# A decoder of two layers on one core: the first cross-attention's exchanged key halves by SBUF transfers, its sums ahead of the mix, two GpSimd memsets later

## The reference, cut to what matters

```python
x = _layernorm(x + _L0_attn_ref(x, ...))
x = _layernorm(x + _L0_xattn_ref(x, ctx_1024, cos, sin, ...))   # here
x = _layernorm(x + _L0_ffn_ref(x, ...))
...
def apply_rope(x, cos, sin):
    d2 = x.shape[-1] // 2
    x1, x2 = (x[..., :d2], x[..., d2:])
    return jnp.concatenate([x1 * cos - x2 * sin, x2 * cos + x1 * sin], axis=-1)
```

## Time and profile before

| | |
|---|---|
| median of 3 runs | 538.3 us (536.81 to 538.79) |
| the profiled execution | 538.49 us, of which the span is 536.7 us |
| PE busy | 426.9 us, 80% of the span |
| DVE, ACT, POOL busy | 317.9, 205.1, 141.0 us |
| mean granted clock of PE | 0.891 |
| the first cross-attention's loop | some 111 to 226 us of the span |

### The profile page before, as it was taken

How to read it: one execution, slowest core, us unless ns; L and a number is a source line. 1 busy time by engine, 2 the same in 40 slices (tenths; PEclk the granted TensorE clock), 3 DMA queues, 4 the chain that set the end, 5 groups by cost and what they waited for, 6 DMA issues and landing times.

```text
span 536.7 us, 6915 instructions
## 1 busy us (share of the span) xinstructions
PE 426.9 (80%) x2568; PEld 247.9 (46%) x2576; DVE 317.9 (59%) x741; ACT 205.1 (38%) x257; POOL 141.0 (26%) x133
## 2 busy tenths in 40 slices
PE   0628957489999999869999558697377989967994
PEld 0306624244444445546777425444133444544484
DVE  4579944627766765551511477863696776225754
ACT  0555613142333233114333348764133445622800
POOL 3205733337777665430000300000100000001500
PEclk9967977889999999978999875999687999985998
DMA  8511000000004111150051250000000000000000
GB/s 317 196 28 42 2 0 1 1 2 0 1 0 158 40 39 40 37 204 2 33 94 26 40 64 5 3 4 1 0 1 2 2 1 3 1 31 0 1 0 21
DMA packets 7358, 19.36 MB, mean 36 GB/s; under 512 B 1750, under 2 KB 3126, under 8 KB 6806
## 3 DMA queue, kind: packets, MB, share of 16 engines
q1 hardware_dynamic: 7324, 18.91, 12.0%
HBM read 17.26 MB, written 1.15 MB: 34 GB/s over the span
## 4 chain that ended last, share of the span: by engine, by line
PE 42%; DVE 26%; POOL 15%; issue 12%; ACT 3%; DMA 1%; POOLq 0%; another core or an unknown queue 0%; DVEq 0%
PE ps L1190 39%; POOL big L540 7%; DVE ps L1043 4%; POOL big L547 4%; POOL rstd L490 2%; DVE mx_a L1047 2%; DVE stats L773 2%; DVE big L866 2%; DVE ps L861 2%; POOL big L522 1%; DVE normed L783 1%; PE ps L1197 1%; DVE x L783 1%; DVE meanvar L776 1%; PE ps L1553 1%
## 5 line engine op out<-in xcount | busy, mean ns | idle before, releaser
L1190 PE MATMUL ps<-big,late 128*32 128x256 f32 (+4 forms) x792 | 103.3, 386 | 13.8 <-DVE mx_x L1043 4.0
L1190 PE MATMUL ps<-late,big 128*128 128x128 f32 (+1 forms) x448 | 64.8, 277 | 3.8 <-DVE mx_x L1043 2.2
L1190 PEld LDWEIGHTS ps<-big,late 128*32 128x32 f32 (+3 forms) x800 | 39.7, 117 | 55.3 <-issue 26.8
L726 ACT ACTIVATE big<-ps 128x1024 f32<-128x1024 f32 x48 | 49.0, 1023 | 39.9 <-PE ps L1190 39.6
L488 POOL TENSOR_SCALAR vareps<-meanvar 128x4 f32<-128x4 f32 (+1 forms) x11 | 2.5, 229 | 224.9 <-DVE meanvar L776 224.9
L1190 PEld LDWEIGHTS ps<-late,big 128*128 128x128 f32 (+1 forms) x448 | 45.0, 152 | 27.3 <-issue 20.6
L664 ACT ACTIVATE big<-ps 128x1024 f32<-128x1024 f32 x32 | 32.8, 1024 | 64.8 <-PE ps L1190 52.9
L540 POOL TENSOR_TENSOR big<-big 128x512 f32<-128x512 f32 x32 | 40.5, 1267 | 43.3 <-DVE big L926 43.3
L1043 DVE CUSTOM_DVE_ANT_0 ps<-ps,big 128x512 f32<-128x512 f32 x64 | 42.6, 717 | 12.2 <-PE ps L1190 9.0
L926 DVE TENSOR_SCALAR big<-big 128x1024 f32<-128x1024 f32 x32 | 25.4, 793 | 39.8 <-ACT big L664 39.8
L1190 PE MATMUL ps<-big 64*128 64x256 f32 (+1 forms) x320 | 47.4, 410 | 1.7 <-POOL big L547 1.0
(11 more groups left out here) (229 smaller groups left out, 655.4 us busy)
## 6 DMA issues: line engine op xcount, KB each, us to landing
attn_w<-in_w_x SPq DMA_DIRECT2D x1, 2560.0 KB, 13.2
big<-parts_kx SPq DMA_DIRECT2D x18, 128.0 KB
late<-in_w_up SPq DMA_DIRECT2D x1, 2048.0 KB, 7.8
late<-in_w_dn SPq DMA_DIRECT2D x4, 512.0 KB, 3.8
attn_w<-in_w_up SPq DMA_DIRECT2D x1, 1024.0 KB, 7.9
attn_w<-in_w_dn SPq DMA_DIRECT2D x1, 1024.0 KB, 10.3
parts_kx<-ctx_r SPq DMA_DIRECT2D x1, 768.0 KB, 3.2
rowv<-in_rowv SPq DMA_DIRECT2D x1, 576.0 KB, 4.3
```

Of the source, the lines that this page charges most:

```text
L726: nc.scalar.activation(ex1[:, n % 3, :].rearrange("p (r n) -> p r n", r=2), ps[:, 2 * (n % 2):2 * (n % 2) + 2, :], ACT.Exp, scale=scale).t ...
L1190: return nc.tensor.matmul(o, lhsT, rhs, start=start, stop=stop, skip_group_check=shared)
```

## The change

1. The keys are projected once. ACT copies the result from PSUM to a new tile `kc` in SBUF. SP's queue then moves it, by four transfers of 32 rows, into `kt2` with neighbouring blocks of 32 rows exchanged (q to q ^ 1). DVE makes the cosine product from PSUM as before, and the sine product in place on `kt2`, now with both inputs in SBUF. POOL's addition stays. `project0` has the keys of batch 0 at u = 0, the query at u = 1, the keys of batch 1 at u = 2, and nothing at u = 3.
2. The denominators of a batch come one logits step later, ahead of the next mix: (c, 0) at u = 3 and (c-1, 1) at u = 1.
3. The loads of w_up0 and w_dn0 move from SP's queue to ACT's.
4. The two memsets behind post1 wait for `x_k_parts`, which DVE signals after it has split the second cross-attention's keys beside expert 1.
5. Some semaphores are merged.

```diff
         kt2 = big1(3072, [P, 2, CS])
+        kc = mid(4096, [P, 2, CS])
...
-            sp.wait_ge(S["e0_used"], 4 * (NPAIR // 2))
-            sp.dma_start(w_up0, a["w_up0"]).then_inc(ld["e0"], 16)
-            for c in range(NPAIR // 2, NPAIR):
-                e = 2 * c - NPAIR
-                sp.wait_ge(S["e0_used"], 4 * (c + 1))
-                sp.dma_start(w_dn0[:, e:e + 2], a["w_dn0"][:, e:e + 2]).then_inc(ld["dn0"], 16)
+            for n in range(2 * NPAIR):
+                sp.wait_ge(S["k0_copy"], n + 1)
+                if n >= 2:
+                    sp.wait_ge(S["k0_done"], n - 1)
+                for q in range(4):
+                    sp.dma_start(kt2[32 * q:32 * q + 32, n % 2, :],
+                                 kc[32 * (q ^ 1):32 * (q ^ 1) + 32, n % 2, :]
+                                 ).then_inc(S[f"k0_swap{n % 2}"], 16)
...
-                if u in (0, 3) and 2 <= c + 1 < NPAIR or n == 3:
-                    rotated0(c + 1, u // 3)
+                if u in (1, 3) and 2 <= c + 1 < NPAIR or n == 3:
+                    rotated0(c + 1, u // 2)
             root("post1")
+            pool.wait_ge(S["x_k_parts"], PARTS)
             link(nc.gpsimd.memset(sel1, -FAR))
-            pool.wait_ge(S["y0_ps"], 1)
-            nc.gpsimd.memset(half_x[1], 0.0).then_inc(S["x_zero1"], 1)
-            pool.wait_ge(S["x_zero1"], 1)
+            nc.gpsimd.memset(half_x[1], 0.0).then_inc(consts, 1)
+            pool.wait_ge(consts, 10)
...
+                elif kind in ("k0", "k1"):
+                    n = 2 * c + int(kind[1])
+                    act.wait_ge(S["k0_ps"], n + 1)
+                    if n >= 2:
+                        act.wait_ge(S[f"k0_swap{n % 2}"], 64 * (n // 2))
+                    nc.scalar.activation(kc[:, n % 2, :], ps[:, 7, :], ACT.Copy
+                                         ).then_inc(S["k0_copy"], 1)
...
                     if c < NPAIR - 1:
-                        if u == 1:
-                            evac0(c + 1, "q")
+                        if u < 3 and (c or u):
+                            evac0(c + 1, ("k0", "q", "k1")[u])
+                    if c >= NPAIR // 2 and u == 2:
+
+                        act.wait_ge(S["e0_used"], 4 * c)
+                        if c == NPAIR // 2:
+                            act.dma_start(w_up0, a["w_up0"]).then_inc(ld["e0"], 16)
+                        else:
+                            down0(c - 1)
...
-            def rotary(c, b, halves=(0, 1)):
+            def rotary(c, b, half):
 
                 n = B * c + b
-                for i in halves:
-                    dst = (kt1, kt2)[i]
-                    dve.wait_ge(S["k0_ps"], 2 * n + i + 1)
+                if half == 0:
+                    dve.wait_ge(S["k0_copy"], n + 1)
                     if n >= 2:
                         dve.wait_ge(S["k0_done"], n - 1)
-                    nc.vector.tensor_tensor(dst[:, n % 2, :], ps[:, 6 + i, :], rope0[:, i, :],
+                    nc.vector.tensor_tensor(kt1[:, n % 2, :], ps[:, 7, :], rope0[:, 0, :],
                                             ALU.mult).then_inc(S["k0_mul"], 1)
+                else:
+                    dve.wait_ge(S[f"k0_swap{n % 2}"], 64 * (n // 2 + 1))
+                    nc.vector.tensor_tensor(kt2[:, n % 2, :], kt2[:, n % 2, :], rope0[:, 1, :],
+                                            ALU.mult).then_inc(S["k0_mul"], 1)
...
-                    if u == 0 and 2 <= c + 1 < NPAIR:
-                        rotary(c + 1, 0)
-                    elif u >= 2 and c + 1 < NPAIR:
-                        rotary(c + 1, 1, (u - 2,))
+                    if c + 1 < NPAIR and (c or u >= 2):
+                        rotary(c + 1, u // 2, u % 2)
...
-                mm(ps[:, 6 + i, :], w_x0[:, c, i, :], cxnT[:, b * CS:(b + 1) * CS]
+                mm(ps[:, 7, :], w_x0[:, c, 0, :], cxnT[:, b * CS:(b + 1) * CS]
                    ).then_inc(S["k0_ps"], 1)
...
+                if u == 3:
+                    denominators0(c, 0)
+                if u == 1 and c:
+                    denominators0(c - 1, 1)
                 mix0(n)
-                if u == 2:
-                    denominators0(c, 0)
-                if u == 0 and c:
-                    denominators0(c - 1, 1)
```

More of the change, by code:

```diff
@@ L378, in stack_x @@
             heads = slice(HB * half, HB * half + HB)
-            sp.wait_ge(S[f"x_zero{half}"], 1)
+            if half:
+                sp.wait_ge(consts, 10)
+            else:
+                sp.wait_ge(S["x_zero0"], 1)
             for c in range(PARTS * PARTS):
@@ L617, in _, with down0 @@
             act.wait_ge(S["negA"], 1)
+            def down0(c):
+                e = 2 * c - NPAIR
+                act.dma_start(w_dn0[:, e:e + 2], a["w_dn0"][:, e:e + 2]).then_inc(ld["dn0"], 16)
             def evac0(c, kind):
@@ L651, in _ @@
                                      ).then_inc(S["ff_act"], 1)
+            evac0(0, "k1")
             for u in range(V_EARLY, 2 * NPAIR):
                 evac0(u // 2, f"v{u % 2}")
+            evac0(1, "k0")
             to_cols(xT[:], 0, "xT_ps", "xT_done", v("lat_g"), v("lat_b"), 3)
@@ L886, in _ @@
             dve.wait_ge(S["rope_signed"], 1)
-            def rotary(c, b, halves=(0, 1)):
+            def rotary(c, b, half):
                 n = B * c + b
-                for i in halves:
-                    dst = (kt1, kt2)[i]
-                    dve.wait_ge(S["k0_ps"], 2 * n + i + 1)
+                if half == 0:
+                    dve.wait_ge(S["k0_copy"], n + 1)
                     if n >= 2:
                         dve.wait_ge(S["k0_done"], n - 1)
-                    nc.vector.tensor_tensor(dst[:, n % 2, :], ps[:, 6 + i, :], rope0[:, i, :],
+                    nc.vector.tensor_tensor(kt1[:, n % 2, :], ps[:, 7, :], rope0[:, 0, :],
+                                            ALU.mult).then_inc(S["k0_mul"], 1)
+                else:
+                    dve.wait_ge(S[f"k0_swap{n % 2}"], 64 * (n // 2 + 1))
+                    nc.vector.tensor_tensor(kt2[:, n % 2, :], kt2[:, n % 2, :], rope0[:, 1, :],
                                             ALU.mult).then_inc(S["k0_mul"], 1)
             for b in range(B):
-                rotary(0, b)
+                for half in range(2):
+                    rotary(0, b, half)
             def add_and_norm(bank, ready, n, res, name, meanwhile=None):
@@ L918, in normed0 @@
                                         ).then_inc(S["o0_norm"], 1)
-            layernorm("lat", x[:], normed, lambda: rotary(1, 0))
+            layernorm("lat", x[:], normed, lambda: rotary(1, 0, 0))
+            rotary(1, 0, 1)
             for c in range(NPAIR):
@@ L1236, in y_of, with keys0 @@
                 ins.then_inc(S["y_ps"], 1)
-            def keys0(c, b, i):
+            def keys0(c, b):
                 n = B * c + b
                 if n:
-                    pe.wait_ge(S["k0_mul"], 2 * (n - 1) + i + 1)
-                if b == 0 and i == 0:
+                    pe.wait_ge(S["k0_mul"], 2 * (n - 1) + 1)
+                if b == 0:
                     pe.wait_ge(S["v0_done"], V_EARLY if c == 0 else 2 * NPAIR)
-                if b == 1 and i == 0 and c:
-                    pe.wait_ge(S["q0_done"], c + 1)
-                mm(ps[:, 6 + i, :], w_x0[:, c, i, :], cxnT[:, b * CS:(b + 1) * CS]
+                mm(ps[:, 7, :], w_x0[:, c, 0, :], cxnT[:, b * CS:(b + 1) * CS]
                    ).then_inc(S["k0_ps"], 1)
             def project0(c, step):
-                if step == 0:
-                    for i in range(2):
-                        keys0(c, 0, i)
-                elif step == 1:
-                    pe.wait_ge(S["k0_mul"], 2 * B * c + 1)
+                if step == 1:
+                    pe.wait_ge(S["v0_done"], 2 * NPAIR)
+                    if c >= 2:
+                        pe.wait_ge(S["q0_done"], c)
                     mm(ps[:, 6, :], w_x0[:, c, 3, :], xT[:]).then_inc(S["q0_ps"], 1)
-                else:
-                    keys0(c, 1, step - 2)
+                elif step < 3:
+                    keys0(c, step // 2)
             def values0(c, i):
@@ L1296, in _ @@
             to_rows(5, [cv[:, 1, :]], [w_mix[:, 5, :]], "mo_ps")
-            for i in range(2):
-                keys0(0, 0, i)
+            keys0(0, 0)
             to_cols(0, normed, "xT_ps", "ln2")
@@ L1303, in _ @@
                 mm(ps[:, 1 + c, :], w_ff[:, c, :], xT[:]).then_inc(S["ff_ps"], 1)
-            for i in range(2):
-                keys0(0, 1, i)
+            keys0(0, 1)
             pe.wait_ge(S["ff_act"], FF)
@@ L1353, in denominators0 @@
                 ins.then_inc(S["o0_ps"], 1)
-            pe.wait_ge(S["k0_mul"], 4)
+            pe.wait_ge(S["k0_mul"], 3)
             for i in range(2):
                 values0(NPAIR - 1, i)
-            for i in range(2):
-                keys0(1, 0, i)
+            keys0(1, 0)
             to_cols(0, normed, "xT_ps", "lat")
```

16 lines of the change are left out of this document (9 added, 7 removed).

## The result

The changed kernel took 550.5 us (median, 548.6 to 551.1), the kernel before 538.5: ratio 1.022, 95% interval 1.0191 to 1.025. It is 11.9 us slower, where 3.4 us faster was predicted, and that lies outside the range.

What follows compares the result with a forecast made beforehand. It took PE's own queue to bound the loop, 14.2 us a pair. Loop +0.2, weights +1.0, ahead of the loop -0.5 and memsets -4.1 sum to -3.4: from 538.3 to 534.9 us, range 529.0 to 541.0.

Steps and rivals of the forecast that it cites:

- The loop: First cross-attention's loop: less PE work against new waits for the clip, +0.2 us, bounds -4.7 and +4.1; weights +1.0 apart.
- PE's own work: Loop: single key projections replace doubles, -12.5 us; PE's work per pair falls from 14.2 to 12.3.
- PE waits for the clip: Loop: PE's mix waits for DVE's clip behind the transfers, 1.95 us a pair, last 1.0, together +12.7.
- weights beside the swap: Loop: w_up0 and w_dn0 loads share DMA engines with the key transfers, +1.0 us; bounds 0 and half of 7.8.
- rival 4: Loop: PE's work falls and its clock with it, so the remaining 12.3 us takes longer and nothing is gained; chance 0.02.
- The transfers: Loop's key chain: four SBUF transfers in a row, 3 x 0.6 issue plus 1.8 landing, taken as 3.7 us.
- the port: Loop: DVE's sine product with two SBUF inputs is held by POOL's adds, 0.7 us taken; bounds 0 and 1.27.
- Rival 2: Loop: every product waits a full POOL add of 1.27 us; loop +4.1, kernel 538.8, no measurable change; chance 0.17.
- Ahead of the loop: Before the loop: post0 sum +1.4 us later, lat normalization 1.9 shorter, together -0.5.
- Denominators: Loop: denominators one logits step later, ahead of the mix, cost nothing on PE and give POOL's totals about 1.5 us more.
- The memsets: Behind the loop: x's normalization without memsets beside it -3.3 us, higher PE clock behind it -0.8, sum -4.1.
- Rival 3: Loop: transfers beyond 3.7 us cost PE in seven pairs; at 4.55 the kernel takes 541, slower than before; chance 0.11.

Runs made afterwards that it cites:

- the three kernels: The kernel before (538.5 us), the changed kernel (550.5 us), and the changed kernel with batch 1's sine product a tile later (528.9 us).
- the late product: Changed kernel with batch 1's sine product and POOL's add behind it moved from u = 3 to the next pair's u = 0: 528.9 us, ratio 0.9824.
- two queues: Changed kernel with two of the four transfers of a key tile issued by ACT behind its copy, two by SP: 530.5 us, ratio 0.9837.

## Why the prediction was wrong

**The loop: +15.9 instead of +1.2** (+0.2 and the +1.0 for the weights). Its terms, by the windows of the three kernels:

| term | predicted | measured |
|---|---|---|
| PE's own work | -12.5 | -11.2 (116.00 to 104.84) |
| PE waits for the clip | +12.7 | +14.6 (6 x 2.17 + 1.58) |
| weights beside the swap | +1.0 | +5.5 (5.93 + 3.92 - 2 x 2.17) |
| lower clock | 0 | +7.5 (112.31 - 104.84) |

They sum to 16.4; the remaining 0.5 is PE's wait of 0.6 for a clip that the kernel before had and the changed one has not. The kernel with the denominators back was 2.3 to 3.4 faster than the change; the table has no row for that, as no trace shows where it arises.

**The step that failed: rival 4, dismissed on the wrong row.** The prediction's sum has PE's work at the higher level throughout, with nothing for the clock; it cost 7.5. I gave 0.02 to a falling clock because the second attention holds 1.00 with PE busy 8.82 of 10, "less densely than here". That was misread: the prediction's own new period has PE busy 12.3 of 14.25 (12.3 and the wait of 1.95), 0.86 and not more than 0.88. And the row is a mean; it says nothing of how long one gap is. The longest gap in that window is 1.05, about half of the predicted one. The same trace had better rows. Behind the hole in which PE waited for x the clock was 0.52, and the prediction used it for the memsets, but not for the seven new holes that it had put into the loop. And at the loop's end stands a single gap of nearly the length of the new ones, 2.32, ahead of eight matmuls of the same shape as eight that ran without a gap 6 us earlier:

```profile
222.79 1.16 PE L1190 MATMUL ps<-attn_w,big 128*128 128x128 f32 x8
...
228.93 2.08 PE L1190 MATMUL ps<-attn_w,big 128*128 128x128 f32 x8 [2.32 <-DVE big L917]
```

Behind it the eight took 2.08 instead of 1.16, at clock 0.50. One such row gives no rate: the changed kernel has the same gap at the same place, and there the eight took 1.16. In the loop the pairs with and without a drop had the same work and the same wait. What the kernels with the late product and with two queues have in common is that PE's waits for the clip are shorter: 0.55 at most with the late product (and one of 1.41 for POOL), 1.6 with two queues. It was not what the rival said ("its work falls, and its clock with it") either: the work fell as much in the late version, and the clock held. With the waits filled by matmuls it held too. The waits did it. Why some waits of 2.17 are followed by a drop and others are not stays open.

**The weights: a term that was mis-sized, +1.0 for +5.5.** My upper bound was half of the load's 7.8. The product started 8.5 after the copy, when the load had just landed, and a piece of w_dn0 (512 KB) did it again for 3.92 - 2.17 = 1.75. The next piece held the last set too: its product started 5.11 after the copy, and PE's wait was 1.58 where the kernel with the weights in pieces has 1.24. Cut into pieces and issued a tile earlier, the load left PE's waits at 2.17 in the profiled execution. The Trainium skill, DMA: Bandwidth & Descriptors, "Queues, rings and completion order", says that a DMA engine takes turns between its queues packet by packet. By that alone one might expect a transfer of 64 KB to be through long before a load of 2 MB, but the packets need not be alike: from 182 to 192 us the load's queue moved 2.10 MB in 144 packets, SP's queue 0.46 MB in 331. No run here shows the order in which they were served; the measured 7.3 of the slowest transfer decides.

**The wait: right in mechanism and place, 2.17 instead of 1.95.** The chain is as it was laid out. The transfers took 3.89 behind the copy instead of 3.7, and the port 0.88 instead of 0.7. Rival 2's picture, in which every product meets a POOL add, was nearer to the trace than a chance of 0.63, though its price of 1.27 was not reached: in three of the four pairs ahead of the load the product arrived 0.20 to 0.24 after the start of a POOL add, and in the fourth 0.98 after it, and each time it ended some 0.55 after that add, so that PE's wait was 2.15 to 2.17 in all four. POOL's add sets the end, and it comes round with the same period; the mean over random arrivals (0.45) was the wrong tool. The 0.7 taken in its place was a guess between two bounds, and that it came near was in part luck.

**Ahead of the loop: +0.4 instead of -0.5.** The lat normalization took 1.1 as predicted, but the sum of post0 came 2.3 later, not 1.4. I counted ACT's copy from the end of DVE's old wait (90.64). It began at 91.41, since the key step itself came later on PE, and the transfers took the same 3.89.

**Denominators.** Put at nothing; the run with the old order was 2.3 (medians) to 3.4 us (ratios) faster, so that the new order costs something. Where, is open.

**The memsets: right.** -3.7 behind the loop for -4.1, and -2.9 (-4.0 to -1.8) as an edit alone; the normalization of x 1.12 for 1.12.

**Rival 3** (slower by the transfers) has the sign, and part of the cause: a set of four did take more than 3.7, but only the three that met a load took much more (8.5, 6.5 and 5.1 from the copy's end to the product, 3.89 elsewhere ahead of the loads), and with the weights in pieces the kernel was still slower (ratio 1.007).

## What to carry to other kernels

When an in-order engine gets a product that waits for a transfer, put it behind everything that another engine waits for: here one tile later turned 12 us lost into 9.5 gained, with the same work. Price every new gap of TensorE twice, once as a wait and once as the clock behind it, and look for a row with a single gap of that length, not for a mean busy share. Small transfers on the path and a large load should not be issued together: issue the small ones first, or split the load, and look that no piece meets them.

## What was not expected of the hardware

- TensorE, back from a wait of 2.17 us, ran at 1.2 GHz in three of four cases in the changed kernel and in two of six with the weights in pieces, though it was busy 12.5 of 14.6 us of each pair: 1.5 us lost for each drop. With surplus matmuls in the gap (0.25 us left of it) no drop was seen.
- A set of four 64 KB transfers issued 0.6 us behind a 2 MB load on another queue let its product start 8.5 us after the copy, when the load had just landed; 3.9 was usual without a load. The slowest transfer of the run took 7.3 us, the median one 2.0.
- A DVE product with two SBUF inputs that starts 0.24 us behind a POOL add takes 1.57 us; with its second input in PSUM 0.69. When the product is first, POOL's add takes 1.66 instead of 1.27.
